# Count matrices of a graph kernel: eight targets a group and two groups a step, with one-hots of the sources made by joint 16-bit operations

## The reference

```python
x = _layernorm(x + _L0_gnn_ref(x, edge_index, L0_gnn_gamma), axis=-1)
x = _layernorm(x + _L1_gnn_ref(x, L1_gnn_qW, L1_gnn_kW, L1_gnn_vW, src, dst), axis=-1)
x = _layernorm(x + _L2_gnn_ref(x, L2_gnn_weights, L2_gnn_loop_w, L2_gnn_bias, src, dst, edge_type_8), axis=-1)
x = _layernorm(x + _L3_gnn_ref(x, ..., src, dst), axis=-1)
```

## Time and profile before

| | us |
|---|---|
| median of 3 runs | 2617.56 |
| the profiled execution, its own time | 2616.92 |
| its span, first to last instruction | 2615.2 |
| counts stage, all but its first and last tile | 18.43 for a tile of 8 windows |

### The profile page before, as it was taken

How to read it: one execution, slowest core, us unless ns; L and a number is a source line. 1 busy time by engine, 2 the same in 40 slices (tenths; PEclk the granted TensorE clock), 3 DMA queues, 4 the chain that set the end, 5 groups by cost and what they waited for, 6 DMA issues and landing times. The chain is left out here.

```text
span 2615.2 us, 63495 instructions
## 1 busy us (share of the span) xinstructions
PE 2291.1 (88%) x21713; PEld 1759.1 (67%) x21714; DVE 2146.3 (82%) x4727; ACT 1175.5 (45%) x2286; POOL 535.5 (20%) x936
## 2 busy tenths in 40 slices
PE   3999999899999999757776676899999899999897
PEld 1555555499999999512111112699999599999887
DVE  8999999965656566689999998799888699988645
ACT  2888888722333233579999996200000400000223
POOL 1111111100000000110000000466664166665000
PEclk9999999999999999889999997999999899999799
DMA  2333333210101010321111112332222432322620
GB/s 67 132 123 140 133 133 141 116 66 27 39 28 39 27 39 2 99 65 42 41 41 42 43 42 108 137 83 72 82 71 37 193 83 72 84 69 57 234 89 20
DMA packets 95192, 206.49 MB, mean 79 GB/s; under 512 B 21620, under 2 KB 61172, under 8 KB 94880
## 3 DMA queue, kind: packets, MB, share of 16 engines
q1 hardware_dynamic: 80544, 182.38, 19.9%
q0 software_dynamic: 14464, 21.44, 4.5%
HBM read 118.17 MB, written 84.76 MB: 78 GB/s over the span
## 5 line engine op out<-in xcount | busy, mean ns | idle before, releaser
L1797 PE MATMUL l_bank<-tab,mask 128*128 128x192 f16 x7600 | 654.0, 247 | 37.6 <-issue 28.6
L1797 PEld LDWEIGHTS l_bank<-tab,mask 128*128 128x128 f16 x7600 | 629.7, 98 | 58.0 <-issue 56.3
L1385 DVE TENSOR_SCALAR mask<-code 128x1600 int32<-128x1600 int32 x304 | 538.2, 1811 | 77.0 <-PE l_bank L1797 40.6
L1769 POOL DMA_INDIRECT ggot<-table_dram,gidx x432 | 411.4, 952 | 240.9 <-issue 84.4
L1268 DVE SCALAR_TENSOR_TENSOR pr<-ex,cring 128x1568 f32<-128x1568 f32 x200 | 356.3, 1782 | 10.7 <-DMA cring<-c_dram 10.7
L1214 PE MATMUL att_acc<-pr,v 128*32 128x392 f32 x1600 | 183.3, 531 | 149.4 <-DVE pr L1268 139.7
L817 PE MATMUL sums<-onehots,ct 128*128 128x192 f16 x3125 | 269.4, 251 | 13.1 <-issue 6.8
L817 PEld LDWEIGHTS sums<-onehots,ct 128*128 128x128 f16 x3125 | 265.7, 100 | 16.7 <-issue 10.6
L817 PE MATMUL sums<-u,ct 128*128 128x192 f16 x3125 | 259.1, 246 | 0.0
L817 PEld LDWEIGHTS sums<-u,ct 128*128 128x128 f16 x3125 | 258.0, 98 | 0.0
L1242 ACT ACTIVATE ex<-score_rest,poss 128x1176 f32<-128x1176 f32 x200 | 249.3, 1246 | 2.9 <-PE score_rest L1206 2.9
(11 more groups left out here) (343 smaller groups left out, 2938.6 us busy)
## 6 DMA issues: line engine op xcount, KB each, us to landing
code<-code_dram SPq DMA_DIRECT2D x38, 800.0 KB
code_dram<-flat SPq DMA_DIRECT2D x100, 200.0 KB, 1.9
ct_dram<-ct SPq DMA_DIRECT2D x25, 800.0 KB, 3.6
c_dram<-flat SPq DMA_DIRECT2D x25, 800.0 KB, 3.3
ct_again<-ct_dram SPq DMA_DIRECT2D x25, 800.0 KB, 16.9
cring<-c_dram SPq DMA_DIRECT2D x200, 98.0 KB, 1.9
table_dram<-tab SPq DMA_DIRECT2D x50, 384.0 KB, 2.3
flat<-code_dram SPq DMA_DIRECT2D x19, 800.0 KB, 4.3
```

The source lines that it names most:

```text
L1385: e.tensor_scalar(turned.rearrange("p (s q d) -> p s q d", q=NQ, d=DQ // 2), words.rearrange("p (q s d) -> p s q d", q=NQ, d=DQ // 2), abs ...
L1769: e.indirect_dma_start(ggot[:, k, j, :], None, table_dram[:, :], bass.IndirectOffsetOnAxis(ap=gidx[:, k, j:j + 1], axis=0)).then_inc(s_ggo ...
L1797: mm = e.matmul(acc[k][:, 0:2 * D], mask[:, r % MR, s, :], tab[:, s, r, :], start=(r == 0 and s == 0), stop=(r == R - 1 and s == NT - 1))
```

## The change

- **Windows.** A group now belongs to SW = 8 targets, so `hot` is WC = 200 wide and a group has GRP = 3 chunks. A step handles two such groups (PAIR = 6 chunks), so that it still covers 16 targets, and there are still 8 windows a tile. The halves of a window write to columns 0 to 199 and 200 to 399 of the same bank.
- **Source one-hots.** `srchot` is now made by VectorE, for all six chunks by one `tensor_tensor` of 768 elements per partition (is_equal of a fixed pattern of lanes with the lanes of the edges), and `codehot` by a second one (`srchot` times the values). All operands are f16. The chunks lie in pairs, interleaved element by element, so that each operand's innermost dimension has two adjacent elements. TensorE's weights are then read with a step of two elements (`chunk_of`).
- **Target one-hots** stay one `tensor_scalar` a chunk: six of 200 in place of five of 400.
- **ScalarE** no longer makes Sign; its two copies out of PSUM stay.
- **GpSimd** reads two first chunks from the table, and has four small operations a step in place of two. It waits for the last VectorE operation of the step two windows back (`s_code`).
- **TensorE**: the counts come first, then the codes; clearing is two matmuls of 2 columns, and one more of 2 columns ends a window and tells ScalarE (`s_full`).
- **Setup**: the table has 16 entries a tile. The marks of which chunk reaches which window are made by 13 `tensor_scalar` of 400 elements in f16 and a tree of `tensor_tensor` max for each side, in place of three operations of 2600 f32 elements; the turned halves are 16 transposes each, and the reductions behind them are twice as long.

```diff
+SW = DW // 2
+WPS = P // SW
+NWS = NP // SW
+WC = NT * SW
+GRP = 3
+PAIR = 2 * GRP
...
+            starts = onehots[0:QROW, 0:NWS]
+            best = lent[0:QROW, NWS // 2:NWS // 2 + 2 * NWS].rearrange("q (k t w) -> q k t w", k=2, w=WPS)
...
-                    c(e.tensor_tensor(hit, bc(cmm[:, :, 1]), bw(wstart[:]), ALU.is_ge))
-                    c(e.tensor_tensor(hit, hit, bc(cbwd[:]), ALU.mult))
-                    c(e.tensor_reduce(halves(0), hit, AX_X, ALU.max))
-                    c(e.tensor_scalar(wstart[:], wstart[:], float(DW), None, ALU.add))
-                    c(e.tensor_tensor(hit, bc(cmm[:, :, 0]), bw(wstart[:]), ALU.is_lt))
-                    c(e.tensor_tensor(hit, hit, bc(cfwd[:]), ALU.mult))
-                    c(e.tensor_reduce(halves(1), hit, AX_X, ALU.max))
-
+                    c(e.tensor_scalar(cmm[:, :, 0], cmm[:, :, 0], -float(SW), None, ALU.add))
+
+                    def reached(k, bound, compare, weight):
+                        for at in range(GCH):
+                            ins = e.tensor_scalar(hits[:, k, at, :], starts, bound[:, at:at + 1], weight[:, at:at + 1],
+                                                  compare, ALU.mult)
+                        c(ins)
+
+                    def most_of(k):
+                        left = GCH
+                        while left > 2:
+                            half = left // 2
+                            c(e.tensor_tensor(hits[:, k, 0:half, :], hits[:, k, 0:half, :], hits[:, k, left - half:left, :], ALU.max))
+                            left -= half
+                        c(e.tensor_tensor(halves(k), hits[:, k, 0, :], hits[:, k, 1, :], ALU.max))
+
+                    reached(0, cmm[:, :, 1], ALU.is_le, cbwd)
+                    most_of(0)
+                    FIRST_HALF[0] = c.n
+                    reached(1, cmm[:, :, 0], ALU.is_gt, cfwd)
+                    most_of(1)
+                    FIRST_HALF[1] = c.n
...
-                        e.wait_ge(s_dve, FIRST_HALF + 4 * k)
-                        for w in range(WPT):
+                        e.wait_ge(s_dve, FIRST_HALF[k])
+                        for w in range(WPS):
...
+            sel = wqk[:, 114:114 + 2 * PAIR].bitcast(F16).rearrange("p (k c g) -> p k c g", k=2, c=2)
+            col = wqk[:, 134:134 + 2 * PAIR].rearrange("p (k g) -> p k g", k=2)
             s_col = sem("cnt_col")
-            codehot = onehots[:, 0:2 * GRP * P].rearrange("p (k g s) -> p k g s", k=2, g=GRP)
+            twos = lambda v: v.rearrange("p (k g s c) -> p k g s c", k=2, g=GRP, c=2)
+            codehot = twos(onehots[:, 0:2 * PAIR * P])
             words = [flat[:, a:b] for a, b in ((0, NP // 2), (NP // 2, NP // 2 + NT * DQ), (NP // 2 + NT * DQ, NP))]
-            srchot = words[2].bitcast(BF16)[:, 0:2 * GRP * P].rearrange("p (k g s) -> p k g s", k=2, g=GRP)
-            hot = onehots[:, 2 * GRP * P:].rearrange("p (k g c) -> p k g c", k=2, g=GRP)
-            zero = sb("cnt_zeros", [P, WC], BF16)
+            srchot = twos(words[2].bitcast(F16)[:, 0:2 * PAIR * P])
+            hot = onehots[:, 2 * PAIR * P:2 * PAIR * (P + WC)].rearrange("p (k j c) -> p k j c", k=2, j=PAIR)
+            chunk_of = lambda v, k, j: v[:, k, j // 2, :, j % 2]
+            zero = onehots[:, NT * 2 * D:NT * 2 * D + P]
...
-                    e.sem_inc(s_hot, 1)
+                    e.sem_inc(s_code, 1)
...
-                                first = load(e, tile_tab[0:1, bass.ds(t, 1), w], 0, 2 * NCHP - GRP)
-                                chunk = nc.s_assert_within(e.snap(g * GRP + first), 0, 2 * NCHP - GRP,
-                                                           skip_runtime_bounds_check_because="the table's first chunk leaves room for all groups")
-                                e.wait_ge(s_hot, e.snap(free) + 1)
-                                e.tensor_tensor(col[:, w % 2, :], edge_col[:, bass.ds(chunk, GRP)],
-                                                woff[:, bass.ds(t * WPT + w, 1)].to_broadcast([P, GRP]),
-                                                ALU.add).then_inc(s_col, 1)
-                                e.tensor_copy(sel[:, w % 2, :, :], edge_sv[:, bass.ds(chunk, GRP), :]).then_inc(s_sel, 1)
+                                chunks = []
+                                for h in range(2):
+                                    first = load(e, tile_tab[0:1, bass.ds(t, 1), 2 * w + h], 0, 2 * NCHP - GRP)
+                                    chunks.append(nc.s_assert_within(
+                                        e.snap(g * GRP + first), 0, 2 * NCHP - GRP,
+                                        skip_runtime_bounds_check_because="the table's first chunk leaves room for all groups"))
+                                e.wait_ge(s_code, e.snap(free) + 1)
+                                for h in range(2):
+                                    ins = e.tensor_copy(sel[:, w % 2, :, h * GRP:(h + 1) * GRP],
+                                                        edge_sv[:, bass.ds(chunks[h], GRP), :].rearrange("p g c -> p c g"))
+                                ins.then_inc(s_sel, 1)
+                                for h in range(2):
+                                    ins = e.tensor_tensor(col[:, w % 2, h * GRP:(h + 1) * GRP], edge_col[:, bass.ds(chunks[h], GRP)],
+                                                          woff[:, bass.ds(t * WPS + (2 * w + h), 1)].to_broadcast([P, GRP]), ALU.add)
+                                ins.then_inc(s_col, 1)
...
+                    every = lambda v, m: v.unsqueeze(1).to_broadcast([P, GRP, m, 2])
+                    each = lambda v, m: v.rearrange("p (g c) -> p g c", c=2).unsqueeze(2).to_broadcast([P, GRP, m, 2])
...
-                                for j in range(GRP):
-                                    ins = e.tensor_scalar(codehot[:, k, j, :], iota[:, 0:P], sel[:, k, j, 0:1],
-                                                          sel[:, k, j, 1:2], ALU.is_equal, ALU.mult)
-                                ins.then_inc(s_code, 1)
+                                e.tensor_tensor(srchot[:, k, :, :, :], every(iota[:, 0:2 * P].rearrange("p (s c) -> p s c", c=2), P), each(sel[:, k, 0, :], P),
+                                                ALU.is_equal).then_inc(s_one, 1)
                                 e.wait_ge(s_col, e.snap(n) + 1)
-                                for j in range(GRP):
-                                    ins = e.tensor_scalar(hot[:, k, j, :], iota[:], col[:, k, j:j + 1],
-                                                          None, ALU.is_equal)
+                                for j in range(PAIR):
+                                    ins = e.tensor_scalar(hot[:, k, j, :], iota[:, 2 * P:2 * P + WC], col[:, k, j:j + 1], None, ALU.is_equal)
                                 ins.then_inc(s_hot, 1)
+                                e.wait_ge(s_one, e.snap(n) + 1)
+                                e.tensor_tensor(codehot[:, k, :, :, :], srchot[:, k, :, :, :], each(sel[:, k, 1, :], P),
+                                                ALU.mult).then_inc(s_code, 1)
...
-                            e.matmul(bank[:, b, 0:WC], zero[:, 0:P], zero[:], start=True, stop=False, skip_group_check=True)
+                            e.matmul(bank[:, b, 0:2], zero, zero[:, 0:2], start=True, stop=False, skip_group_check=True)
                         with e.Fori(0, groups):
-                            e.wait_ge(s_hot, e.snap(n) + 2)
-                            for j in range(GRP):
-                                e.matmul(codes[:, b, 0:WC], codehot[:, k, j, :], hot[:, k, j, :],
+                            e.wait_ge(s_hot, e.snap(n) + 1)
+                            for j in range(PAIR):
+                                h = j // GRP
+                                e.matmul(counts[:, b, h * WC:(h + 1) * WC], chunk_of(srchot, k, j), hot[:, k, j, :],
                                          start=False, stop=False, skip_group_check=True)
-                            e.wait_ge(s_one, e.snap(n) + 1)
-                            for j in range(GRP):
-                                mm = e.matmul(counts[:, b, 0:WC], srchot[:, k, j, :], hot[:, k, j, :],
+                            e.wait_ge(s_code, e.snap(n) + 2)
+                            for j in range(PAIR):
+                                h = j // GRP
+                                mm = e.matmul(codes[:, b, h * WC:(h + 1) * WC], chunk_of(codehot, k, j), hot[:, k, j, :],
                                               start=False, stop=False, skip_group_check=True)
                             mm.then_inc(s_used, 1)
                             e.reg_add(n, n, 1)
+                        e.matmul(codes[:, b, 0:2], zero, zero[:, 0:2], start=False, stop=True, skip_group_check=True).then_inc(s_full, 1)
...
-                    def ones(w, groups):
-
-                        e.reg_mov(past, n)
-                        with e.Fori(0, groups):
```

(17 more changed lines are left out.)

83 lines of the change are left out of this document (37 added, 46 removed).

## The result

The changed kernel takes 2583.99 us (median of four runs, 2580.72 to 2585.94) where the kernel before takes 2616.51 (median of four): a ratio of 0.9871 with an interval of 0.9851 to 0.9891. The forecast was 2593. The profiled execution takes 2582.09 us with a span of 2580.4, so 34.8 us less than the one before. Lines of the kernel before keep their work and move: L432 has become L460 and L467, L437 is L464, L510 and L514 are L545 and L540, L407 and L410 are L435 and L431, L341 is L358, L817 is L838.

The account below looks back on a forecast made before the run. VectorE's queue bounds the stage before, GpSimd's 17.5 us a tile after. Setup 0, first step +0.4, tiles −23, end −1.2: −24 us against 2616.92 gives 2593; range from 2566, with 4 us for fixed-cost bounds, to 2632.

Parts of the forecast that it names:

- VectorE's step: VectorE in the stage: two joint operations and six target one-hots, 2.03 us in place of 2.29; 16.4 us a tile.
- GpSimd's round: GpSimd's sequencer in the stage: 1.89 us a round with the second table read; 17.5 us a tile in all, above VectorE's.
- slow reads: GpSimd's table reads while both 800 KB stores run: three or four a tile, 1.5 to 1.9 us.
- Setup: Setup work on VectorE's queue: net 0 us (−1 to +1; +5 if 16-bit pairs are no faster).
- first step: Start of the stage: the first step waits for the second table read, +0.4 us.
- the tail: End of the stage: the last window's matmuls end 1.2 us sooner behind VectorE, and what follows hangs on them.
- (a): GpSimd keeps up in the stage: VectorE's 16.4 us a tile holds, 51 us saved, 2566 us; chance 0.21.
- (b): GpSimd and VectorE hold each other up in the stage: a tile of 19.6 us, +29 us, 2645; chance 0.16.
- the sign: GpSimd's small operations in the stage: the forecast is wrong if L410's successors last over 0.5 us in the mean.
- (c): VectorE's joint operations run at one element a clock: step 2.83 us, tile 22.8, 2730 us in all; chance 0.05.
- (d): TensorE, less used, falls to 1.2 GHz: a tile of 20.2 us, +44 us, 2661 in all; chance 0.05.
- almost nowhere: Expected sign in the stage: GpSimd hardly ever waits for VectorE, while VectorE idles 1 us a tile, ended by GpSimd.

Follow-up runs that it names:

- the split kernel: Against the kernel with packed table and one joint target one-hot operation of 1200 elements: that operation split into 800 and 400; 2530.64 us, ratio 0.9666.
- the unused read: Kernel before the change plus a second table read per GpSimd round, value unused; the read isn't in the program, only a register move; 2617.36 us, ratio 0.9999.
- the packed table: Changed kernel with both first chunks of a round packed into one table entry, read once, separated by mask and shift; 2557.48 us, ratio 0.9773.

## Why the prediction was right

**VectorE's step** (2.03 us) came out as summed: 0.47 and 0.181 us, 2.02 a step. Two elements a clock was the choice between far bounds; (572 − 359) / 400 = 0.53 ns an element, in the split kernel, confirms it over another width. The Trainium skill ("VectorE: DVE Perf Modes", the perf-mode tier table) gives that rate for 16-bit `tensor_tensor`, and the trace agrees.

**GpSimd's round** decided, and its sum holds term by term: a free round of 1.84 us (1.89 predicted), 0.72 for the outer loop (0.7; 2.56 us of the round that ends with the copies at 304.58, less 1.84), and slow reads of 2.0 us a tile (1.7), the sum of what each read takes beyond 0.275, 34.3 us from 140 to 440. 8 × 1.84 + 0.72 + 2.0 = 17.4 of 17.50. With joint target one-hots the same sum is 14.7 + 0.72 + 1.46 = 16.9, the 16.92 that was measured. That the second read and the stores together make it is shown by taking away each, and that the sequencer is the bound by its never waiting for VectorE. The tile came out to the hundredth by luck: the round was summed 0.4 us a tile too long and the slow reads 0.3 too short.

**The whole** is 9 us under the forecast by the median, 11 by the profiled executions, for reasons outside the steady tile. The first tile and the last two gave 7.8 us where 25 × 0.93 had counted 2.8; that VectorE waits for a TensorE at half clock in the last tile of before was in view and not counted. Setup and first step gave 0.5 us where they were to cost 0.4; the tail gave 0.2 and not 1.2. And the propagation gave 6.6 us that nothing had forecast. Setup by itself came out as summed. Its second half:

```profile
21.58 3.91 DVE L267 TENSOR_SCALAR ct<-onehots,cmm,cfwd 124x400 f16<-124x400 f16 x13
25.52 2.83 DVE L275 TENSOR_TENSOR ct<-ct 124x2400 f16<-124x2400 f16 x3
28.39 0.57 DVE L277 TENSOR_TENSOR onehots<-ct 124x400 f32<-124x400 f16 x1
29.00 2.21 DVE L291 TENSOR_REDUCE ct<-setup_turned 25x16 f32<-25x1984 f32 x1
```

That is 29.00 − 21.58 = 7.4 us for a side (7.4 predicted), and 2.21 in place of 1.18 for the reduction behind it.

**The propagation.** The stage takes 537.4 us before and 530.8 after, counted from the first matmul's start to the last one's, with 6250 matmuls in both. The largest part of the difference is TensorE's clock. Between the phases of the propagation TensorE pauses three times, and behind each of these pauses the clock is at 0.50, its lower level of 1.2 GHz, for 6.8, 3.4 and 6.8 us in the kernel before. In the changed one it is at 1.00 behind two of them and at 0.50 for 3.4 us behind one. This is the stretch from the first phase change on, before and after:

```profile
634.33:641.13 6.80, 6.05 (x38) 5.38 (x39) 0.95 (x3) 0.37 (x1) 0.00 (x0) 0.50 0.02 5
```

```profile
605.01:611.81 6.80, 6.80 (x72) 6.20 (x73) 1.92 (x6) 1.56 (x3) 0.00 (x0) 1.00 0.02 5
```

At half clock a matmul follows the other after 0.160 us in place of 0.082. There are 118 such intervals (over 0.14 us) in the stage before and 52 after, which is 9.3 and 4.1 us above the short ones: 5.2 of the 6.6 us. The half clock at the stage's start, for its first 5.8 and 4.2 us, is in these.

The rest is in pauses. From matmul to matmul the three take 2.3 to 3.0 us in every kernel. In the kernel before, and in its variant with the unused read, a second pause of 0.9 to 1.5 us follows each; in none of the eleven kernels with the change in them is there one. That variant and then the changed kernel, TensorE's timeline:

```profile
632.32 1.83 PE L818 MATMUL sums<-onehots,ct 128*128 128x192 f16 x14 [2.09 <-DVE onehots L884]
635.08 1.61 PE L818 MATMUL sums<-onehots,ct 128*128 128x192 f16 x12 [0.93 <-issue]
```

```profile
605.01 4.19 PE L838 MATMUL sums<-onehots,ct 128*128 128x192 f16 x38 [2.44 <-issue]
```

The variant has this second pause at full clock here, so half clock doesn't make it. All pauses together are 2.5 us longer before; smaller intervals give 1.1 back. The stage takes 537.4 and 537.1 us in the first two kernels, and 530.1 to 532.7 in the others; the two longest, 532.5 and 532.7, are at half clock behind all three phase changes, for 3.4 us each. The second pauses wait for nothing that the profile shows. What in the changed program removes them, and keeps the clock up, was not tried: it stays open, and 6.6 of the 34.8 us with it.

**The rivals.** (a), GpSimd keeps up: this would have been right without the slow reads; taking the stores or one read away gives a tile of 16.2 us, near its 16.4. (b), GpSimd and VectorE in each other's way: the mechanism exists, its price is on the other side. GpSimd's operation waits for VectorE's: one of the two that begin at 304.98 above takes 0.65 us, and from 140 to 440 us each of the 106 that take over 0.4 us ends within 0.12 us behind a joint operation of VectorE. One joint operation still starts 0.47 us behind another where it waits for nothing; where VectorE's next operation needs what the held one makes, it comes late (0.64 us in 52 of 136 steps). L431 and L435 last 0.30 us in the mean, under the 0.5 that I had set as the sign. The Trainium skill ("SBUF — State Buffer", Who interferes with whom) states an exclusive lock between such operations; the traces agree in that GpSimd waits for whole operations with two inputs and hardly for `tensor_scalar` (0.22 us with the packed table). They show no joint operation of VectorE that GpSimd held; what VectorE lost was the wait for a late result. In the changed kernel GpSimd's round hides it; in the packed one, with the small loss between the `hot` operations, it is 0.3 us a tile. (c) and (d) did not come: `srchot` took 0.55 us, and the clock was 1.00 in the tile.

**Signs.** GpSimd waiting for VectorE "almost nowhere" was wrong as the profile counts it (104 us), and right by the sequencer, whose gaps ahead of the wait never exceed 52 ns from 140 to 440 us.

## What to carry to other kernels

An engine that is idle for most of a loop can still be its next bound through its sequencer: add up what it issues in one round, reads into registers first, and compare that with the period after the change, not before. A faster bound engine is worth only the distance to that sum, here 0.93 us a tile of the 2.2 that VectorE's own step would give (18.43 − 16.21). Whether a sequencer is the bound shows in the gap ahead of its wait, not in the idle time that the profile puts down to another engine. When it then binds, look for fewer entries read, not for fewer reads.

## What was not expected of the hardware

- A read of two neighbouring table entries into registers takes 0.52 us, two single ones 2 × 0.28; a mask and a shift on a packed entry are cheaper (rounds of 1.64 in place of 1.84 us).
- Such a read takes up to 0.90 us beside 800 KB stores and at most 0.37 us without (66 to 440 us).
- GpSimd's small copies take 0.22 us beside `tensor_scalar` and 0.50 in the mean beside gapless `tensor_tensor`. VectorE's joint operations don't start later for it, but one that needs the held operation's result does (0.646 us behind the last one in place of 0.469).
- TensorE's clock was at 0.50 for 17.0 us behind the three phase changes of the propagation before, and for 3.4 to 10.2 us in the kernels with the change; matmuls of 192 columns then follow each other after 0.160 us in place of 0.082.
- Weights with a stride of two elements cost TensorE nothing (matmuls of 200 columns follow each other after 0.086 us, with weights in one run as with these), a moving operand with that stride 0.004 us.
